# A fused attention and expert decoder on one core: in the first half of each slot, ScalarE takes the last half-slot's units out ahead of the exp instead of behind it

## The chip, the cores and the metric

The kernel runs on one core of one Trainium2 chip. The metric is the device time of one execution in microseconds (us). Three executions of the kernel before were timed; a fourth was profiled.

## The reference

The input is a batch of 8 sequences of 512 rows and 256 features, `x`, and a context of the same shape. Three layers follow each other, each with `x = layernorm(x + layer(x))`:

- a linear attention with a decaying state (decay 0.99, rate 0.01) of 128 features, which the kernel computes as a masked product of queries and keys;
- a cross attention on the context, with 16 heads of 16 features, softmax over 512 keys;
- a sum of a self attention of the same shape and a mixture of 8 experts (256 by 256 each), of which the two with the largest gate count.

All of it is float32.

## The kernel before, in words

Each sequence needs two softmax attentions of 16 heads: a cross attention (phase "C") and a self attention (phase "S"). `PHASES` puts the 16 phases in one row, and everything else is woven between them: the projections, layer norms, linear attention and experts of one sequence run while the softmax of another does. A phase is cut into 16 slots (4 groups of 4 heads, by 4 blocks of 128 keys), so there are 256 slots, and a slot has two halves, `h = 0` and `h = 1`, of two heads each. Time is counted in half-slots `t = 2 * s + h`; it starts at negative values, for the work that precedes the first softmax. "First half" below is `h = 0`, "second half" is `h = 1`.

Every engine runs its own loop over the same `t`, and issues its work in program order:

- TensorE (line 643 on): in each half the scores of two heads (`scores`: two matmuls side by side into the one buffer `sc`, which first wait for the exp of the half before, since `sc` is not doubled), then two matmuls for the row maxima of a slot six ahead (`max_tiles`, into `mx`, three banks in turn). In the first half follow the products of the last slot's probabilities with the values (`values`, eight matmuls into `op`). In the second half follow the **units**: all matmuls of everything that isn't softmax, each filling one of the two banks of `ms`.
- ScalarE (line 767 on): in each half the exp of the scores (`exps`, 128x1024, out of `sc` into `probs`, line 721), then the taking out of the units that carry the number of the half before (`UNITS.get(t - 1)`), then other tasks (`OTHERS["act"]`: the copy of `op` into `oT`, the last step of layer norms `apply01` and `apply23`, the gate's exp).
- VectorE: the maxima of `mx` (line 884), its own share of the units, layer norm statistics, the choice of experts. It takes the low part of the projections that are split into two (`low`, line 794), after ScalarE has made the high part (`high`, line 660).
- GpSimd adds the experts' outputs up (line 1051); SyncE issues the DMAs.

The order of units is written out by hand in the tables `LIN...`, `MID...` and `MOE...`: each name has a slot and a half. At most two units stand in one half. TensorE computes the units of both halves of a slot at one place, at the end of the slot's second half: first those with half 0, then those with half 1. ScalarE takes the units with half 0 out in the same slot's second half, behind that half's exp. It takes those with half 1 out in the first half of the next slot. The units with half 1 that ScalarE takes out are what the change moves. By the tables they stand in 148 of the 256 slots:

- one of the 16 expert units of a sequence (`moe`: 6 matmuls; taken out by two activations of 128x256 with a scale per row, line 714, into `moe`): 67 slots with that unit alone; in 14 more a `heads` unit (four transposes, VectorE takes them out) follows it on TensorE, in 6 `hT1` and in 6 `combT` (four transposes each, which ScalarE takes out with one copy, line 659);
- a projection of 128x512 that is taken out with a bias (`q1`, `k1`, `qc0`, `qc1`, `kc0`, `kc1`, `q3c0`, `q3c1`, `k3c1`, line 660): 42 slots with that unit alone (26 with four float32 matmuls, 16 with six float32r ones), 4 more with `heads` behind it;
- a copy of 128x512 alone (`o1`, `hT1`, `x2T1`, line 659): 9 slots.

A unit may only overwrite its bank of `ms` when the unit two before it has been taken out (`wait_unit_out` at the head of `unit`). An expert unit's taking out also waits until GpSimd has added the entry two before it (`acc`).

Of the kernel before, what the change touches and what calls it, by code (L numbers as in the profile page):

```python
# [37 lines left out]
PHASES = [("C", 0)] + [ph for n in range(B - 1) for ph in (("C", n + 1), ("S", n))] + [("S", B - 1)]  # L38
PHASE = {ph: p for p, ph in enumerate(PHASES)}
SLOTS = G * TB  # L40
# [59 lines left out]
def lin_at(task, n):  # L100

    slot, half = lin_table(n)[task]
    return 2 * (slot + (start_of("C", n) if n >= 2 else 0)) + half
# [111 lines left out]
def decoder(nc, x, xT, ctxT, w, out):  # L215
    with ExitStack() as ctx:
# [92 lines left out]
        def unit_bank(unit):  # L309
            return ms[:, PLACE[unit] % 2, :]  # L310

        def wait_unit(eng, *unit):

            eng.wait_ge(ms_t[PLACE[unit] % 2], PLACE[unit] // 2 + 1)
# [341 lines left out]
        def _(act):  # L656
            def copy(dst, src, bias=None):
                if bias is None:
                    return nc.scalar.activation(dst, src, ACT.Copy)  # L659
                return nc.scalar.activation(dst, src, ACT.Identity, bias=bias, scale=1.0)  # L660

            def high(task, n):

                name, c = task[0], int(task[-1])
                e = half_stack(task, n)
                bias = {"kc": W["bk2"], "qc": bq2, "k3": W["bk3"], "q3": bq3}[task[0:2]]
                if e >= 1:
                    act.wait_ge(stack_in[name], 16 * TERMS * SIDES * e)
                wait_unit(act, task, n)
                copy(part[name][:, 0, :].bitcast(F32R), unit_bank((task, n)), bias[:, c:c + 1]).then_inc(part_high[name], 1)  # L670

            def take_out(task, n):

                bank = unit_bank((task, n))
                done = ms_out[PLACE[task, n] % 2]
                if task in ("q1", "k1"):
                    if n >= 1:
                        wait_unit(act, "qc1", n - 1)
                    wait_unit(act, task, n)
                    copy(q1T if task == "q1" else k1T, bank, W["b" + task][:, 0:1]).then_inc(done, 1)  # L680
                elif task == "o1":
                    wait_unit(act, task, n)
                    copy(o1T[:], bank).then_inc(done, 1)
                elif task in ("x0", "x1"):
                    wait_unit(act, task, n)
                    copy(x1T[:, int(task[1]), :], bank).then_inc(done, 1)
                elif task in ("hT0", "hT1"):
                    wait_unit(act, task, n)
                    copy(headsT[:, int(task[2]), :], bank).then_inc(done, 1)
                elif task in ("x2T0", "x2T1"):  # L690
                    wait_unit(act, task, n)
                    copy(x2T_part[0][:, int(task[3]), :].bitcast(F32R), bank).then_inc(x2_high, 1)
                elif task == "gate":
                    wait_unit(act, task, n)
                    copy(gateT, bank[:, 0:P]).then_inc(done, 1)
                elif task == "combT":
                    wait_unit(act, task, n)
                    copy(combT, bank[0:E, :]).then_inc(done, 1)
                elif task in ("be0", "be1"):
                    k = ENTRY[task, n]  # L700
                    wait_unit(act, task, n)
                    if k >= 2:
                        act.wait_ge(acc, 2 * (k - 1))
                    copy(moe[:, k % 2, :], bank).then_inc(moe_out, 2)
                elif task.startswith("moe"):
                    k = ENTRY[task, n]
                    t, pair = int(task[3:]) // (E // 2), int(task[3:]) % (E // 2)
                    wait_unit(act, task, n)
                    act.wait_ge(g_step, G_STEPS * (n + 1))
                    if k >= 2:  # L710
                        act.wait_ge(acc, 2 * (k - 1))
                    for j in range(2):
                        e = 2 * pair + j
                        nc.scalar.activation(moe[:, k % 2, j * D:j * D + D], bank[:, j * D:j * D + D], ACT.Copy,  # L714
                                             scale=comb[:, t, e:e + 1]).then_inc(moe_out, 1)

            def exps(s, h):
                act.wait_ge(score, 2 * s + h + 1)
                if s - 1 + h >= 1:
                    act.wait_ge(pv, s - 1 + h)  # L720
                nc.scalar.activation(probs[:, (2 * s + h) % 3, :, :], sc[:], ACT.Exp).then_inc(exp_out, 1)  # L721

            def other(task, k, n):
                if task == "oT":
                    act.wait_ge(pv, TB * (k + 1))
                    if k >= 1:
                        wait_unit(act, "heads", k - 1)
                    copy(oT[:], op[:]).then_inc(oT_out, 1)
                elif task in ("apply01", "apply23"):
                    src, dst = ((x_s, x1), (x1b, x2[:, n % 2]))[k]  # L730
                    if k == 0 and n >= 1:
                        act.wait_ge(x1b_out, n)
                    if k == 1 and n == 0:
                        act.wait_ge(we_cut, 2 * DC)
                    if k == 1 and n >= 2:
                        act.wait_ge(y_out, 16 * (n - 1))
                    act.wait_ge(ln_step[k], LN_STEPS[k] * (n + 1))
                    for t in (0, 1) if task == "apply01" else (2, 3):
                        nc.scalar.activation(dst[:, t, :], src[:, t, :], ACT.Identity, bias=drop[:, k, t:t + 1],
                                             scale=rstd[:, k, t:t + 1]).then_inc(ln_out[k], 1)  # L740
                else:
                    act.wait_ge(g_step, G_STEPS * n + 3)
                    nc.scalar.activation(g_e[:], g_l[:], ACT.Exp).then_inc(g_exp, 1)
# [7 lines left out]
            for t in range(FIRST_HALF, LAST_HALF + 1):  # L751
                s, h = t // 2, t % 2
                if t == lin_at("y01", 0):
                    act.wait_ge(w_late, 16 * len(LATE))
                    nc.scalar.mul(bq2[:], W["bq2"][:], HD ** -0.5).then_inc(scaled, 1)
                    nc.scalar.mul(bq3[:], W["bq3"][:], HD ** -0.5).then_inc(scaled, 1)
                    nc.scalar.mul(W["wq2"][:], W["wq2"][:], HD ** -0.5).then_inc(scaled, 1)
                    act.wait_ge(w3_in, 16 * 2)
                    nc.scalar.mul(w3_stage[0][:, :, 0:D], w3_stage[0][:, :, 0:D], HD ** -0.5).then_inc(scaled, 1)
                    act.wait_ge(scaled, 4)  # L760
                if t == 2 * -12:
                    act.wait_ge(we_in, 16 * DC)
                    for c in range(DC):
                        copy(we_part[0][:, c, :].bitcast(F32R), we_stage[c]).then_inc(we_cut, 1)
                    for k in range(2):
                        copy(w3_part[0][:, :, W3_COLS[k]].bitcast(F32R), w3_stage[k]).then_inc(w3_cut, 1)
                if t == 0:
                    act.wait_ge(we_cut, 2 * DC)
                    act.wait_ge(w3_cut, 4)
                if 0 <= s < SLOTS * len(PHASES):  # L770
                    exps(s, h)
                for task, n in UNITS.get(t - 1, []):
                    if task in SPLITS:
                        high(task, n)
                    else:
                        take_out(task, n)
                for task, k, n in OTHERS["act"][t]:
                    other(task, k, n)
                if t == lin_at("qc0", 0) + 1:
                    act.wait_ge(fills, 5)  # L780
                    act.wait_ge(part_low["q"], 1)
                    for i in range(TERMS):
                        act.dma_start(qs[64 + HD * i:64 + HD * i + HD, 0, :, :],
                                      part["q"][64:128, Q_PART[i], :]).then_inc(stack_in["q"], 16)
# [346 lines left out]
```

## Time and profile before

| | |
|---|---|
| Three timed executions | 1293.77, 1296.06 and 1296.37 us, median 1296.06 us |
| Profiled execution | 1295.17 us, of which the span from the first to the last instruction is 1293.4 us |
| Granted TensorE clock, mean | 0.981 of full speed |
| TensorE matmul busy | 1224.4 us, 95% of the span |
| VectorE, ScalarE, GpSimd busy | 911.8, 776.9 and 348.4 us (70%, 60%, 27%) |
| Instructions | 19863 |

A busy time is a sum over the instructions of one engine, with overlaps counted once. Matmul ends are modelled. A row of the timeline gives the start in us from the span's start, the duration in us, the engine (PE is TensorE's matmuls, PEld its weight loads, ACT is ScalarE, DVE VectorE, POOL GpSimd), the line, the operation, the tiles as out<-in, their shapes and how many instructions are merged, and in brackets the idle time of the engine ahead of it and what ended that.

### The profile page before, as it was taken

Reading aid. Unit: us, or ns where it says so; the run is one execution under the profiler, and the core shown is the slowest. Engines: PE = TensorE matmul, PEld = TensorE weight load, DVE = VectorE, ACT = ScalarE, POOL = GpSimd, SP = SyncE. Lnnn points to the kernel's source line nnn. Section 1 sums busy time; section 2 is a strip of 40 time slices with the busy share of each in tenths; the row PEclk is TensorE's granted clock in tenths of the full one; section 3 lists DMA queues with packets and bytes.
Section 4 is the critical chain, followed back from the end, with each engine's and each line's share of the span. In section 5 each row is a group of like instructions: output and inputs, shape, how many; then the busy total and the mean of one; then the engine's idle time right before and its main releaser. Section 6 shows DMA issues by size and latency. Waiting matters only on the chain.

```text
span 1293.4 us, 19863 instructions
## 1 busy us (share of the span) xinstructions
PE 1224.4 (95%) x6912; PEld 603.1 (47%) x6912; DVE 911.8 (70%) x1825; ACT 776.9 (60%) x1081; POOL 348.4 (27%) x421
## 2 busy tenths in 40 slices
PE   7789989999999999999999999999999999997995
PEld 4333344454554445554554545544454444453542
DVE  5467777557776787767877687767777677767762
ACT  2235555656567665757657666676657576665664
POOL 2410012230622206211333206121152114420262
PEclk9879998999999999999999999999999999998998
DMA  6913324223334133333422243341323333303300
GB/s 234 146 28 63 60 33 59 49 27 73 61 67 67 23 72 57 67 51 50 83 43 58 35 83 51 66 67 26 60 49 51 51 51 51 67 2 51 50 19 17
DMA packets 50243, 74.92 MB, mean 58 GB/s; under 512 B 8536, under 2 KB 20320, under 8 KB 49888
## 3 DMA queue, kind: packets, MB, share of 16 engines
q1 hardware_dynamic: 48896, 72.72, 32.2%
q10 hardware_dynamic: 1248, 0.92, 0.4%
q8 instruction: 57, 0.93, 0.4%
q14 instruction: 42, 0.34, 0.1%
HBM read 18.04 MB, written 4.19 MB: 17 GB/s over the span
## 4 chain that ended last, share of the span: by engine, by line
PE 78%; DVE 9%; ACT 5%; issue 4%; DMA 2%; SPq 1%; POOL 0%; ACTq 0%; DVEq 0%
PE ms L422 36%; PE op L422 15%; PE sc L422 15%; PE mx L422 8%; DVE maxes L884 4%; ACT probs L721 2%; PE ms L527 2%; DMA qs<-q_parts 2%; PE ms L472 1%; ACT moe L714 1%; DVE ks L974 1%; SPq L370 1%; PE ms L522 1%; DVE x1b L835 1%; DMA qs<-shift_r 1%
## 5 line engine op out<-in xcount | busy, mean ns | idle before, releaser
L884 DVE TENSOR_REDUCE maxes<-mx 128x1 f32<-128x512 f32 x1024 | 657.7, 684 | 274.1 <-PE mx L422 272.1
L721 ACT ACTIVATE probs<-sc 128x1024 f32<-128x1024 f32 x512 | 524.9, 1025 | 390.7 <-PE sc L422 384.3
L1051 POOL TENSOR_TENSOR x<-x,moe 128x256 f32<-128x256 f32 x256 | 187.2, 731 | 688.4 <-ACT moe L714 668.5
L422 PE MATMUL op<-probs,v 128*32 128x512 f32 x2048 | 276.2, 612 | 1.7 <-ACT probs L721 1.1
L422 PE MATMUL sc<-qs,ks 50*128 50x512 f32 x1024 | 258.6, 502 | 15.8 <-ACT probs L721 10.2
L422 PEld LDWEIGHTS sc<-qs,ks 50*128 50x128 f32 x1024 | 96.2, 184 | 316.8 <-ACT probs L721 235.0
L422 PE MATMUL mx<-ks,qs 48*128 48x512 f32 x1024 | 208.8, 403 | 11.3 <-DVE maxes L884 6.7
L714 ACT ACTIVATE moe<-ms,comb 128x256 f32<-128x256 f32 x256 | 107.1, 473 | 27.3 <-PE ms L422 27.3
L422 PEld LDWEIGHTS mx<-ks,qs 48*128 48x128 f32 x1024 | 98.7, 189 | 17.8 <-DVE maxes L884 11.2
L422 PE MATMUL ms<-we_hi,x2T_hi 128*128 128x512 f32 x256 | 94.5, 450 | 3.0 <-DVE x1b L835 1.9
L422 PEld LDWEIGHTS op<-probs,v 128*32 128x32 f32 x2048 | 40.5, 108 | 95.7 <-issue 94.3
L422 PE MATMUL ms<-we_lo,x2T_hi 128*128 128x512 f32 x256 | 80.9, 397 | 0.0
L422 PE MATMUL ms<-we_hi,x2T_lo 128*128 128x512 f32 x256 | 80.9, 397 | 0.0
L422 PEld LDWEIGHTS ms<-we_hi,x2T_hi 128*128 128x128 f32 x256 | 39.5, 191 | 36.9 <-issue 17.4
L422 PEld LDWEIGHTS ms<-we_lo,x2T_hi 128*128 128x128 f32 x256 | 48.7, 190 | 11.5
L422 PEld LDWEIGHTS ms<-we_hi,x2T_lo 128*128 128x128 f32 x256 | 48.4, 189 | 11.7
L794 DVE SCALAR_TENSOR_TENSOR k_parts<-ms,w_bk,k_parts 128x512 fp32r<-128x512 f32 x32 | 24.0, 751 | 39.2 <-ACT k_parts L660 38.7
L1011 POOL TENSOR_SCALAR var<-mv 128x4 f32<-128x4 f32 x24 | 5.6, 234 | 146.8 <-DVE mv L915 146.1
L527 PE MATMUL ms<-w_ident,oT 128*128 128x128 f32 x256 | 39.7, 278 | 1.3 <-ACT oT L659 0.8
L660 ACT ACTIVATE k_parts<-ms,w_bk 128x512 fp32r<-128x512 f32 x32 | 22.0, 687 | 28.8 <-PE ms L422 28.8
L527 PEld LDWEIGHTS ms<-w_ident,oT 128*128 128x128 f32 x256 | 29.9, 141 | 19.9 <-DVE shift_r L848 12.5
L659 ACT ACTIVATE oT<-op 128x512 f32<-128x512 f32 x64 | 38.1, 596 | 1.2 <-PE op L422 1.2
(123 smaller groups left out, 1241.9 us busy)
## 6 DMA issues: line engine op xcount, KB each, us to landing
ks<-k_parts SPq DMA_DIRECT2D x192, 128.0 KB, 4.4
qs<-q_parts SPq DMA_DIRECT2D x189, 128.0 KB, 4.6
xT_s<-in_xT SPq DMA_DIRECT2D x8, 512.0 KB, 3.8
x_s<-in_x SPq DMA_DIRECT2D x8, 512.0 KB, 4.1
ctxT_s<-in_ctxT SPq DMA_DIRECT2D x8, 512.0 KB, 3.8
out<-x SPq DMA_DIRECT2D x7, 512.0 KB, 2.9
qs<-shift_r SPq DMA_DIRECT2D x128, 8.0 KB
probs<-in_we SPq DMA_DIRECT2D x1, 1024.0 KB, 7.2
```

Of the source, the lines that this page charges most:

```text
L370: sp.dma_start(dst[at:at + HD, e % RING, :, :], part[name][64 * side:64 * side + 64, which[r], :]).then_inc(stack_in[name], 16)
L422: return nc.tensor.matmul(dst, lhsT, rhs, start=first, stop=last, skip_group_check=True)
L472: last = nc.tensor.transpose(bank[:, t * P:(t + 1) * P], src[:, t, c * P:(c + 1) * P], ident[:])
L522: last = nc.tensor.transpose(bank[0:SHIFT * HG * TB, 0:P], shift_n[:, n % 2].rearrange("p s a m -> p (s a m)"), ident[:])
L527: last = nc.tensor.transpose(bank[:, t * P:t * P + P], oT[:, t * P:t * P + P], ident[:])
L659: return nc.scalar.activation(dst, src, ACT.Copy)
L660: return nc.scalar.activation(dst, src, ACT.Identity, bias=bias, scale=1.0)
L714: nc.scalar.activation(moe[:, k % 2, j * D:j * D + D], bank[:, j * D:j * D + D], ACT.Copy, scale=comb[:, t, e:e + 1]).then_inc(moe_out, 1)
L721: nc.scalar.activation(probs[:, (2 * s + h) % 3, :, :], sc[:], ACT.Exp).then_inc(exp_out, 1)
L794: nc.vector.scalar_tensor_tensor(out=part[name][:, 1, :].bitcast(F32R), in0=unit_bank((task, n)), scalar=bias[:, c:c + 1], in1=part[name][ ...
L884: nc.vector.tensor_reduce(maxes[:, g % 2, at:at + 1], mx[:, i % 3, :], AX_X, ALU.max).then_inc(max_out, 1)
L1051: nc.gpsimd.tensor_tensor(x2[:, n % 2, t, :], x2[:, n % 2, t, :], moe[:, k % 2, j * D:j * D + D], ALU.add).then_inc(acc, 1)
```

## The change

In the first half of each slot the loop of ScalarE takes the units of the last half-slot out first and issues the exp behind them. In the second half the order stays: exp, then units. The other tasks stay behind both. No other engine's program changes.

```diff
@@ -767,13 +767,15 @@
                 if t == 0:
                     act.wait_ge(we_cut, 2 * DC)
                     act.wait_ge(w3_cut, 4)
-                if 0 <= s < SLOTS * len(PHASES):
+                if h == 1 and 0 <= s < SLOTS * len(PHASES):
                     exps(s, h)
                 for task, n in UNITS.get(t - 1, []):
                     if task in SPLITS:
                         high(task, n)
                     else:
                         take_out(task, n)
+                if h == 0 and 0 <= s < SLOTS * len(PHASES):
+                    exps(s, h)
                 for task, k, n in OTHERS["act"][t]:
                     other(task, k, n)
                 if t == lin_at("qc0", 0) + 1:
```

## Rows read from the trace of the kernel before

**Rows 1.** The chain that ended last, shares of the span by engine.

```profile
PE 78%; DVE 9%; ACT 5%; issue 4%; DMA 2%; SPq 1%; POOL 0%; ACTq 0%; DVEq 0%
```

**Rows 2.** Waits, whole span: total us, times, longest.

```profile
POOL x L1051 <- ACT moe L714: 668.5, 100, 33.4
...
PEld sc L422 <- ACT probs L721: 235.0, 286, 1.5
...
PEld ms L422 <- DVE q_parts L794: 10.2, 16, 3.4
```

**Rows 3.** Timeline, slot 57: its first half, an expert unit ahead of it.

```profile
359.98 0.63 PE L422 MATMUL ms<-we_lo,x2T_hi 128*128 128x512 f32 x2
...
360.54 0.50 PE L422 MATMUL sc<-qs,ks 50*128 50x512 f32 x2
...
361.09 1.02 ACT L721 ACTIVATE probs<-sc 128x1024 f32<-128x1024 f32 x1 [1.40 <-PE sc L422]
...
361.21 1.07 PE L422 MATMUL op<-probs,v 128*32 128x512 f32 x8
...
362.01 0.84 ACT L714 ACTIVATE moe<-ms,comb 128x256 f32<-128x256 f32 x2
...
362.21 0.50 PE L422 MATMUL sc<-qs,ks 50*128 50x512 f32 x2
```

**Rows 4.** Timeline, slot 254, near the end: a first half without max matmuls.

```profile
1275.36 1.06 PE L422 MATMUL op<-probs,v 128*32 128x512 f32 x8
1275.47 1.02 ACT L721 ACTIVATE probs<-sc 128x1024 f32<-128x1024 f32 x1 [0.60 <-PE sc L422]
...
1276.55 0.50 PE L422 MATMUL sc<-qs,ks 50*128 50x512 f32 x2
```

**Rows 5.** Timeline, slot 51: ScalarE waits for an expert unit of half 0.

```profile
334.03 0.62 PE L422 MATMUL ms<-we_lo,x2T_hi 128*128 128x512 f32 x2
...
334.69 0.84 ACT L714 ACTIVATE moe<-ms,comb 128x256 f32<-128x256 f32 x2 [0.81 <-PE ms L422]
```

**Rows 6.** Timeline, slot 34: ScalarE waits for a projection of half 0.

```profile
249.37 1.45 PE L422 MATMUL ms<-ctxT_s,w_wk 128*128 128x512 f32 x3
...
250.92 0.69 ACT L660 ACTIVATE k_parts<-ms,w_bk 128x512 fp32r<-128x512 f32 x1 [1.21 <-PE ms L422]
```

**Rows 7.** Timeline, slot 48: a projection of half 1, taken out behind the exp.

```profile
314.79 1.98 PE L422 MATMUL ms<-xT_s,w_wk 128*128 128x512 f32 x4
...
318.17 0.68 ACT L660 ACTIVATE x1T<-ms,w_bk 128x512 f32<-128x512 f32 x1
...
318.74 0.23 ACT L743 ACTIVATE g_e<-g_l 128x32 f32<-128x32 f32 x1
```

**Rows 8.** Timeline, slot 69: an expert unit and hT1, both of half 1.

```profile
413.73 0.63 PE L422 MATMUL ms<-we_lo,x2T_hi 128*128 128x512 f32 x2
...
414.20 0.60 PE L472 MATMUL ms<-w_ident,heads 128*128 128x128 f32 x4
...
416.19 0.83 ACT L714 ACTIVATE moe<-ms,comb 128x256 f32<-128x256 f32 x2
...
416.90 0.61 ACT L659 ACTIVATE lin<-ms 128x512 f32<-128x512 f32 x1
...
417.38 1.05 ACT L721 ACTIVATE probs<-sc 128x1024 f32<-128x1024 f32 x1
```

**Rows 9.** Timeline, slot 63: the late exp of the second half, and the scores behind it.

```profile
391.01 1.03 ACT L721 ACTIVATE probs<-sc 128x1024 f32<-128x1024 f32 x1
...
391.24 0.63 PE L422 MATMUL ms<-we_lo,x2T_hi 128*128 128x512 f32 x2
392.09 0.49 PE L422 MATMUL sc<-qs,ks 50*128 50x512 f32 x2 [0.22 <-ACT probs L721]
```

**Rows 10.** Timeline, slot 229: layer norm steps behind the taking out of an expert unit.

```profile
1164.49 2.07 ACT L739 ACTIVATE x<-x1b,drop,rstd 128x256 f32<-128x256 f32 x4
...
1166.70 1.06 PE L472 MATMUL ms<-w_ident,x 128*128 128x128 f32 x8 [1.99 <-ACT x L739]
```

## The prediction

> **What bounds the kernel now.** I read the chain that ended last first: 78% of it is TensorE, 5% ScalarE [rows 1]. The waits come next: TensorE's weight loads for scores waited 286 times for an exp, 235.0 us in total, and that is its largest wait [rows 2]. A weight load can wait while the matmuls ahead of it still stream, so only a timeline tells whether this is lost time.
>
> The timeline of a first half [rows 3] has the whole cycle. Write S for the start of its scores, 360.54. The exp starts at S+0.55 and ends at S+1.57, and the scores of the second half start at S+1.67. The value matmuls between them are modelled to end at 362.28. The same rows show where scores start when TensorE alone decides: 0.07 before the modelled end of the matmuls ahead (expert unit: end 360.61, scores 360.54). By this TensorE is free at 362.21, which is when the second scores start. Near the end of the kernel the row maxima are finished, and the value matmuls end earlier (at 1276.42, so TensorE is free at 1276.35); there the scores start at 1276.55, 0.06 after the exp's end of 1276.49 [rows 4]. From the exp's start to the scores this takes 1.08, in slot 57 1.12. So in the first half **two limits lie 0.04 to 0.05 apart**: TensorE's own work at S+1.67, and behind it the exp's round trip at S+1.62. An exp later than today by d moves the next scores by d less 0.045. TensorE's program is a fixed row behind these scores, so the slot ends later by the same.
>
> In the second half TensorE has units to compute, usually 1 to 3 us of them, so that exp has room.
>
> **The change, part by part.** *Nothing is added or removed*: the same activations run, and no DMA or semaphore changes its place against another engine's program. Moved are the units of half 1 that ScalarE takes out, in 148 slots; in the other 108 the order stays. They now stand ahead of the exp of the first half, on which the weight loads of the next scores wait; they no longer stand between the first exp and the second.
>
> *When can taking out begin?* An expert unit's activation starts 0.04 after the modelled end of its last matmul (334.65 to 334.69) [rows 5]. One with a bias as a column starts 0.10 after it (250.82 to 250.92) [rows 6]. The unit ends 0.07 past S, since scores start that much ahead of the modelled end. So an expert unit is ready at S+0.11, a projection at about S+0.165, a copy at S+0.11, all before the scores themselves are ready for exp at S+0.545.
>
> *How long does it hold ScalarE?* Two expert activations: 416.19 to 416.90, a step of 0.71. A copy: 416.90 to 417.38, 0.48 up to an exp's start [rows 8]. A projection with bias: 318.17 to 318.74, 0.57 [rows 7].
>
> The Trainium skill ("ScalarE: Activation LUTs", What ACT_TABLE_LOAD costs) gives an activation 186 ns and 0.833 ns per element, 93 ns more for a column operand, and an overlap of 93 ns between neighbours. By it the step of one 256-wide expert activation is an estimated 0.40, so 0.80 for two, where the row has 0.71; the sum below would be about 7 us higher. The measured step is used.
>
> The sum, by kinds of slot (counts from the tables):
> - 67 with an expert unit alone: 0.11 + 0.71 = S+0.82 in place of 0.545, 0.275 later, less 0.045: 0.23 each, 15.4 us.
> - 12 with an expert unit and then hT1 or combT: the expert unit ends at 414.36 and its taking out 0.75 later, at 415.11; the copy takes it to 415.59. S is 414.80 less 0.07, 414.73, so the exp is due at 415.27 and comes 0.32 late [rows 8]. combT is a narrower copy, 0.04 less. About 0.25 each after the cover, 3.0 us.
> - 42 projections alone: 0.165 + 0.57 = S+0.735, 0.19 late, 0.145 after the cover; 41 of them count (one, q1 of the third sequence, ended early because TensorE waited for a DMA), 5.9 us. The unit of rows 7 shows the same: end 316.77, ready 316.87, done 317.44, where the exp was due at 317.25.
> - 9 copies alone: 0.11 + 0.48 = 0.59, 0.045 late, all of it covered: 0.
> - 18 with `heads` behind: the unit ends with 0.44 less, ready at S-0.33, done by S+0.38, before the scores: 0.
>
> That is 24.3 us, and 0.1 more for three slots at the end that have no cover [rows 4].
>
> *What comes back.* The second exp no longer stands behind these units. Where layer norm steps also stood ahead of it, it was late, but it was TensorE's limit in only five slots like slot 63: the exp of 391.01 to 392.04 set the scores at 392.09, while the matmuls ahead end at 391.87, so TensorE would be free at 391.80 [rows 9]. That is 0.29 each, 1.5 us. In slot 229 the four layer norm steps start at 1164.49, and TensorE waits 1.99 for them [rows 10]. Today exp and two expert activations stand ahead of them; then it is the same three, but begun at S+0.11 by the expert pair in place of S+0.545 by the exp. So the steps start 0.435 earlier, and the slot gains this in place of losing 0.23, 0.7 us. High parts done earlier let VectorE's low parts start about 0.1 earlier where TensorE waits for them behind a `heads` unit, four slots, 0.4 us; all such waits of weight loads are 10.2 us, the upper bound [rows 2]. In all 2.6 us.
>
> *Costed at nothing.* VectorE: after its two maxima of a first half it waits for no one but the high part, which comes earlier; the maxima of the second half shift with TensorE. GpSimd: it waits 668.5 us for expert results, so they come earlier into an idle engine [rows 2]; the taking out of a unit waits for the entry two before it, and no row shows ScalarE waiting for that. If that cover were gone, the exp would wait as well: one addition's length each time. SyncE: some stacks of keys and queries can be issued earlier, by at most what VectorE's queue lets through, 0.1. ScalarE's waits now stand ahead of exp: a projection also waits for the DMAs of its predecessor, several slots old.
>
> Sum: 24.4 - 2.6 = **21.8 us more**. The profiled execution took 1295.17, 0.9 under the median of 1296.06. From it follows 1317.0, from the median 1317.9. I forecast 1318.
>
> **The bounds.** If the cover of 0.045 is not there (the row's 362.21 could be the exp's round trip after all, with 0.05 more for a queue), 120 slots cost 0.045 more and the nine copies appear: 1324. If it is twice that, 1312. If taking out can start at the modelled end itself, minus 0.04 to 0.10 a slot, 1311; both together, 1306. If no overlap between activations remained (0.84 + 0.11 for the pair [rows 3], 0.68 for a projection), 0.13 and 0.11 more, 1333.
>
> **The rivals.**
> 1. *Hidden.* The taking out fits between the unit's end and the scores' end, so the exp is not late. For it: ScalarE is idle 1.40 ahead of this exp in slot 57 [rows 3], and busy only 60% of the span. Against it: the idle time lies before S+0.11, when no unit is ready, and only 0.43 remain for a step of 0.71. It would hold if units were ready 0.23 earlier. Then only the gains stand: 1296.06 - 2.6 = 1293.5, within 0.2%. The Trainium skill ("Perfetto Trace Analysis", Identifying the Most-Contended Engine) has the engine with the highest occupancy decide; by that, an order on an engine busy 60% changes nothing. Rows 3 speak against that rule here, since the path passes from scores through exp to scores within a half.
> 2. *Faster.* The late second exps are the price paid today: 12 slots like slot 69 (0.45 late), 12 like slot 63 (0.95), and slot 229 (1.9) are 18.7 us. If TensorE waited in all of them and rival 1's condition holds too, 1277. It decides from the point where a second half's units are shorter than the exp's lateness. Against it: the brackets that name ScalarE stand only in slots like those of rows 9 and 10; in the other 19 of these 25 TensorE still computes units when the late exp ends.
> 3. *Heavier.* The exp behind a taking out does not overlap it and pays a semaphore's delay too: 0.24 more in 79 slots, 0.11 more in 41, 0.12 in the rest, 25 us more, 1343. Rows 8 speak against it: an exp follows a copy with a step of 0.48, where the copy takes 0.61.
>
> **How the numbers follow.** About 0.2% (2.6 us) is what a measurement of this kernel can tell from no change. Forecast 0.80 (1306 to 1328), heavier 0.11, hidden 0.06, faster 0.03. So slower 0.91, same 0.06, faster 0.03. The range is 1308 to 1328: it leaves out the faster and hidden cases, most of the heavier one, and the thin ends of my own.
>
> **What would show it.** In slots with an expert unit alone, the exp of the first half starts 0.82 after the scores, directly behind two activations of line 714, and the next scores at S+1.90 in place of 1.67; with a projection S+1.81; without a unit, or with `heads` behind, S+1.67 as before. The exp of the second half starts 0.55 after its scores in nearly all slots. TensorE's matmul busy time stays near 1224 and its waits for exp grow by some 22 us. Rival 1 would show the exp at S+0.55, rival 3 at S+0.95 or later, and either makes the forecast wrong. So would a row in which ScalarE, ahead of the exp, waits for GpSimd or a DMA.

## The result and the profile after

| | before | after |
|---|---|---|
| Four executions, median | 1296.12 us (1293.77 to 1296.37) | 1313.85 us (1311.09 to 1318.42) |
| Profiled execution / its span | 1295.17 / 1293.4 us | 1311.09 / 1309.2 us |
| ScalarE busy | 776.9 us | 784.7 us |

The ratio is 1.0144, with a 95% interval of 1.0113 to 1.0176. The change makes the kernel 17.7 us slower. Executions at a lower granted clock, one of the kernel before (1363.27 us) and one of the last version below (1871.21 us), are left out of all medians and ratios.

The beginning and the end of an execution differ from run to run: the first scores come between 72.8 and 79.3 us after the start in the ten traces, whatever the order. So I also compare a stretch in which this hardly occurs, called the stretch below: from the first scores of slot 27 to the first scores of slot 229. The windows view gives its bounds and length, and then busy time of TensorE's matmuls, its weight loads, VectorE, ScalarE and GpSimd (instructions in brackets), the granted clock as a share of full speed, and the DMA share and rate. First the kernel before, then the changed one:

```profile
207.18:1162.32 955.14, 942.19 (x5453) 471.04 (x5452) 700.84 (x1421) 611.71 (x861) 276.76 (x343) 1.00 0.32 54
```

```profile
203.36:1175.91 972.55, 946.21 (x5451) 469.49 (x5451) 701.24 (x1421) 616.89 (x861) 276.51 (x343) 1.00 0.32 53
```

The same work at the same full clock takes 17.4 us more, and TensorE is busy in only 4.0 of these.

The chain that ended last, by engine, and four lines of the waits of the changed kernel (total us, times, longest):

```profile
PE 65%; ACT 15%; DVE 11%; issue 7%; DMA 1%; SPq 0%; POOL 0%; ACTq 0%; DVEq 0%
```

```profile
ACT probs L721 <- PE sc L422: 266.0, 336, 6.5
...
PEld sc L422 <- ACT probs L721: 258.7, 282, 1.6
...
ACT moe L714 <- PE ms L422: 86.6, 109, 1.8
...
PE sc L422 <- ACT probs L721: 25.1, 91, 1.1
```

ScalarE's share of the chain went from 5% [rows 1] to 15%, TensorE's from 78% to 65%. The weight loads of scores wait 23.7 us more for an exp than in [rows 2], and the score matmuls themselves 25.1 where it was 10.2 us. The two lines overlap in time and are not to be added. ScalarE waits less for scores than before (it was 384.3 us) and more for expert units (it was 27.3): it now meets a unit first.

The timeline of slot 57, to be laid beside [rows 3]:

```profile
358.83 0.63 PE L422 MATMUL ms<-we_lo,x2T_hi 128*128 128x512 f32 x2
...
359.39 0.50 PE L422 MATMUL sc<-qs,ks 50*128 50x512 f32 x2
...
359.50 0.84 ACT L714 ACTIVATE moe<-ms,comb 128x256 f32<-128x256 f32 x2 [0.97 <-PE ms L422]
...
360.06 1.06 PE L422 MATMUL op<-probs,v 128*32 128x512 f32 x8
360.23 1.02 ACT L721 ACTIVATE probs<-sc 128x1024 f32<-128x1024 f32 x1
...
361.30 0.49 PE L422 MATMUL sc<-qs,ks 50*128 50x512 f32 x2 [0.18 <-ACT probs L721]
```

With S = 359.39, the expert pair starts at S+0.11, the exp at S+0.84 instead of S+0.55, and the next scores at S+1.91 instead of S+1.67. The value matmuls now end at 361.12, 0.18 before these scores. TensorE waits for the exp.

The first half with a projection ahead (slot 48, S = 314.68), where the exp comes at S+0.75 and the next scores at S+1.82:

```profile
314.68 0.50 PE L422 MATMUL sc<-qs,ks 50*128 50x512 f32 x2
...
314.85 0.69 ACT L660 ACTIVATE x1T<-ms,w_bk 128x512 f32<-128x512 f32 x1 [1.59 <-PE ms L422]
...
315.43 1.02 ACT L721 ACTIVATE probs<-sc 128x1024 f32<-128x1024 f32 x1
...
316.50 0.50 PE L422 MATMUL sc<-qs,ks 50*128 50x512 f32 x2
```

And slot 69, with an expert unit and hT1 ahead, beside [rows 8]. Its S is 414.77, so the exp comes at S+0.88 and the next scores at S+1.96:

```profile
414.24 0.60 PE L472 MATMUL ms<-w_ident,heads 128*128 128x128 f32 x4
...
414.44 0.84 ACT L714 ACTIVATE moe<-ms,comb 128x256 f32<-128x256 f32 x2 [0.21 <-PE ms L422]
...
415.17 0.60 ACT L659 ACTIVATE lin<-ms 128x512 f32<-128x512 f32 x1
...
415.65 1.03 ACT L721 ACTIVATE probs<-sc 128x1024 f32<-128x1024 f32 x1
...
416.73 0.50 PE L422 MATMUL sc<-qs,ks 50*128 50x512 f32 x2 [0.23 <-ACT probs L721]
```

**Where the time went, over all slots.** I compared each half of each slot, from scores to scores, between the two traces. In slots with a moved unit the first halves are 25.9 us longer in all and the second halves 7.0 us shorter. The rest (slots without a moved unit, the start, and the second halves of slots 12 and 22, whose waits differ from run to run) is 3.1 us shorter. The sum is 15.8, which is the difference of the two spans.

What the second halves give back has two main sources. The first is the late exp, as in slot 63. Here it starts at 390.05 and no longer sets the scores, which follow the expert unit's modelled end of 391.61 by -0.07 as TensorE does when it decides alone (in [rows 9] they were held until 0.05 after the exp):

```profile
390.05 1.01 ACT L721 ACTIVATE probs<-sc 128x1024 f32<-128x1024 f32 x1
...
390.98 0.63 PE L422 MATMUL ms<-we_lo,x2T_hi 128*128 128x512 f32 x2
...
391.54 0.50 PE L422 MATMUL sc<-qs,ks 50*128 50x512 f32 x2
```

The second I had mostly missed, and slot 68 shows it. Its second half begins at 411.37 before and at 411.69 after. Before:

```profile
411.89 0.75 DVE L794 SCALAR_TENSOR_TENSOR q_parts<-ms,bq2s,q_parts 128x512 fp32r<-128x512 f32 x1
...
412.03 0.66 PE L472 MATMUL ms<-w_ident,heads 128*128 128x128 f32 x4
...
412.69 0.30 PEld L422 LDWEIGHTS ms<-we_hi,x2T_hi 128*128 128x128 f32 x2 [0.24 <-DVE q_parts L794]
412.69 0.72 PE L422 MATMUL ms<-we_hi,x2T_hi 128*128 128x512 f32 x2
```

After:

```profile
411.85 0.74 DVE L796 SCALAR_TENSOR_TENSOR q_parts<-ms,bq2s,q_parts 128x512 fp32r<-128x512 f32 x1
...
412.36 0.65 PE L472 MATMUL ms<-w_ident,heads 128*128 128x128 f32 x4
...
412.77 0.72 PE L422 MATMUL ms<-we_hi,x2T_hi 128*128 128x512 f32 x2
```

The transposes start 0.67 after the second scores in both. The expert unit follows them by 0.66 before and by 0.41 after. It needs the bank that the projection filled, and before the change VectorE's low part still read that bank until 412.64. The low part waits for ScalarE's high part, so when the high part comes earlier the bank does too. Eleven slots gain 0.26 to 0.37 by this, 3.1 us. Slots 250 and 251 gain 0.27 and 0.30 by a bank too: in slot 251 before, the expert unit starts 0.73 after the second scores and its bracket names the taking out of the expert unit ahead (line 714, 0.23 us); after, it starts 0.43 behind them.

**Six pairs that start late.** A unit that is ready at S+0.11 isn't taken out before ScalarE is free. In six of the 67 slots with an expert unit alone, layer norm steps of the half before still hold it. In slot 42 (S = 288.20) the pair starts at S+0.41, the exp at S+1.13, and the half costs 0.55:

```profile
287.63 1.08 ACT L739 ACTIVATE x<-x1b,drop,rstd 128x256 f32<-128x256 f32 x2
...
288.61 0.83 ACT L714 ACTIVATE moe<-ms,comb 128x256 f32<-128x256 f32 x2
...
289.33 1.03 ACT L721 ACTIVATE probs<-sc 128x1024 f32<-128x1024 f32 x1
```

In slot 74 and four like it the pair starts at S+0.18 and the exp at S+0.89, and each costs 0.30.

### The profile page after: what moved, and what is told of

It is laid out like the page before. It is cut to its first block, busy times and chain, and to the rows that moved or that the text cites. A ratio compares the mean times of both kernels' runs of the same rounds, so it can differ in the third digit from the quotient of the medians.

```text
span 1309.2 us, 19863 instructions
## 1 busy us (share of the span) xinstructions
PE 1225.3 (94%) x6912; PEld 598.4 (46%) x6912; DVE 912.0 (70%) x1825; ACT 784.7 (60%) x1081; POOL 348.2 (27%) x421
## 4 chain that ended last, share of the span: by engine, by line
PE 65%; ACT 15%; DVE 11%; issue 7%; DMA 1%; SPq 0%; POOL 0%; ACTq 0%; DVEq 0%
PE ms L422 36%; PE sc L422 12%; ACT probs L721 10%; PE op L422 7%; PE mx L422 6%; DVE maxes L886 5%; ACT moe L714 3%; PE ms L527 2%; PE ms L472 1%; DVE ks L976 1%; PE ms L522 1%; ACT x L739 1%; DMA qs<-q_parts 1%; DMA qs<-shift_r 1%; DVE x1b L837 1%
## 5 line engine op out<-in xcount | busy, mean ns | idle before, releaser
L422 PE MATMUL sc<-qs,ks 50*128 50x512 f32 x1024 | 258.0, 500 | 32.5 <-ACT probs L721 25.1
L422 PEld LDWEIGHTS ms<-we_hi,x2T_lo 128*128 128x128 f32 x256 | 48.2, 188 | 11.5
```

Of the source, the lines that this page charges most:

```text
L422: return nc.tensor.matmul(dst, lhsT, rhs, start=first, stop=last, skip_group_check=True)
```

## The experiments

The reason to be tested: a first half has two limits, 0.04 apart (the cover), and a taking out ahead costs as much as it makes the exp later, less the 0.04. The rivals are that something else in the moved order costs (banks, queues, the second halves), or that these extra microseconds come from other engines.

**Only the expert units ahead.** The other units stay behind the exp. The edit is against the kernel before; `...` marks lines left out of a diff.

```diff
+                units = UNITS.get(t - 1, [])
+                ahead = [u for u in units if h == 0 and u[0].startswith('moe')]
+                for task, n in ahead:
...
                 if 0 <= s < SLOTS * len(PHASES):
                     exps(s, h)
-                for task, n in UNITS.get(t - 1, []):
+                for task, n in units:
+                    if (task, n) in ahead:
+                        continue
```

> Only the expert units go ahead of the exp; the other units of half 1 stay behind it. Theory (round trip): the exp starts when the taking out ends, and only what exceeds a cover of about 0.05 us reaches the next scores. 67 slots with an expert unit alone: exp at S+0.83, next scores at S+1.91, 0.25 us each, 16.6 us; the 26 slots with another unit behind it: 0. Back come 1.5 us in the five slots like 63 and 0.7 of slot 229 (0.25 of it counted above). Span 14 to 15 us over the kernel before. Rival (cost spread over all moved units alike, by disturbance of TensorE or by waits ahead of the exp): 93 of 160 moved units, so about 9 us, and some of it in slots with heads behind the unit.

One execution took 1309.80 us, one of the kernel before 1292.86. The span is 14.6 us over that of the trace before, as the theory had it, and the stretch takes 966.64 us, 11.5 more. The 67 first halves with an expert unit alone have a median of 1.912 with the exp at S+0.835, as with the whole change, and cost 17.25 us together. Those with a projection are back at 1.663 to 1.667. Where hT1 follows the expert unit, the half costs nothing either: the expert pair is out before the scores are, and only the copy behind it, which here stands behind the exp, had delayed the exp.

**All but the expert units ahead.** Against the last one:

```diff
-                ahead = [u for u in units if h == 0 and u[0].startswith('moe')]
+                ahead = [u for u in units if h == 0 and not u[0].startswith('moe')]
```

> All units but the expert units go ahead; these stay behind the exp. Theory (round trip): 41 projections alone cost 0.155 us each, 6.4 us; copies alone, and hT1 or combT behind an expert unit, reach S+0.60 for the exp and cost 0.01. Back come 0.27 in each of the 12 slots after qc0 or qc1 (the next unit's bank is free earlier) and about 0.2 in the four with heads behind the projection, 4 us. Together 2 to 3 us over the kernel before. Rival (cost spread alike over all moved units): 67 of 160, 6 to 7 us.

One execution took 1299.52, the kernel before 1292.86, which is 6.7 less. By itself that would suit the rival. The stretch takes 956.81, only 1.7 more. The span is 4.4 us over the trace before (the traced execution before was itself 2.3 us slower than the 1292.86 here), and 2.4 of these lie in slot 230, where the granted clock was 0.50 from 1168.4 to 1171.5 us in this run and 1.00 in the trace before; there the exp stands at S+0.83 and S+0.84 in the two halves. The projections cost 0.155 to 0.16 each, with the exp at S+0.753 and the half 1.822 long. A copy puts the exp at S+0.60 and costs 0.01. The bank wait of slot 68 is gone here too (-0.27 in ten slots, -0.37 in the one after kc1), and so it belongs to the projections. Together the two runs give 13.2 us in the stretch, the whole change 17.4. What is missing is above all in the slots with two moved units: neither part of the change alone costs anything where hT1 follows an expert unit, but the two together cost 1.8 us there; and of the six slots in which combT follows one, the first part gains 0.28 in four and the second in all six, the whole in one.

**Half an expert unit ahead.** Only the first of its two activations stands ahead of the exp; the second and all other units stay behind.

```diff
+                units = UNITS.get(t - 1, [])
+                split = h == 0 and 0 <= s < SLOTS * len(PHASES) and len(units) > 0 and units[0][0].startswith("moe")
+                if split:
+                    take_out(*units[0], parts=(0,))
                 if 0 <= s < SLOTS * len(PHASES):
                     exps(s, h)
-                for task, n in UNITS.get(t - 1, []):
...
+                for task, n in units:
+                    if split and (task, n) == units[0]:
+                        take_out(task, n, parts=(1,))
```

> Only the first of the two activations of each expert unit goes ahead of the exp; everything else stays as before. Theory (round trip): it ends at S+0.11+0.36 = S+0.47, before the scores are ready for the exp at S+0.545, so the exp and the next scores stay at S+0.545 and S+1.66 in all 67 slots; five slots like 63 gain up to 0.3 and slot 229 gains 0.36: 1 to 2 us under the kernel before. Rival (what is taken out ahead costs in proportion): half of 17 us, 8 us more.

One execution took 1290.60, the kernel before 1292.86; the stretch takes 951.65, 3.5 less than before. Slot 57, S = 359.64:

```profile
359.64 0.50 PE L422 MATMUL sc<-qs,ks 50*128 50x512 f32 x2
...
359.74 0.48 ACT L715 ACTIVATE moe<-ms,comb 128x256 f32<-128x256 f32 x1 [0.97 <-PE ms L422]
...
360.18 1.03 ACT L722 ACTIVATE probs<-sc 128x1024 f32<-128x1024 f32 x1
...
361.10 0.47 ACT L715 ACTIVATE moe<-ms,comb 128x256 f32<-128x256 f32 x1
361.30 0.50 PE L422 MATMUL sc<-qs,ks 50*128 50x512 f32 x2
```

One activation fits between the unit's end and the scores' end: the exp starts at S+0.54 and the next scores at S+1.66. Taking units out ahead costs nothing as long as it ends before the scores do. Slot 42 is the one of the 67 where it doesn't: behind the layer norm steps the single activation puts the exp at S+0.78, and the half costs 0.19. The gains remain: 0.31 in the five slots like 63, 0.36 in slot 229, 0.28 in six combT slots; the last had not been foreseen. This separates the lateness of the exp from everything else that the order changes.

**More of the same cost.** The changed kernel, with one spare copy of 128x96 between the expert pair and the exp in the 67 slots.

```diff
+                    mine = [task for task, _ in UNITS.get(t - 1, [])]
+                    if len(mine) == 1 and mine[0].startswith("moe"):
+                        nc.scalar.activation(spare[:], ident[:, 0:96], ACT.Copy)
                     exps(s, h)
```

> The change, with one more activation (a copy of 128x96 into a spare tile, which nothing reads) between the taking out and the exp in the 67 slots with an expert unit alone. Theory (round trip): past the cover each ns of lateness is one of the slot. The copy takes a step of about 0.17 us, so exp at S+1.0, next scores at S+2.08, 67 times 0.17 = 11 us over the changed kernel, all of it in these first halves. Rival (TensorE has work to fill, the first halves stretch less than the exp is late): under 6 us.

One execution took 1329.37, the kernel before 1292.86. The 67 first halves have a median of 2.084, 0.172 more than with the change alone, 11.5 us in all, which is what the theory asked for. The stretch, in which 56 of them lie, takes 981.04, 8.5 more than with the change alone (9.6 in these halves, less 1.1 that combT slots gain). The whole execution is longer by more because its first scores came 6.4 us later, ahead of everything that the edit touches. Slot 57, S = 368.03:

```profile
368.03 0.50 PE L423 MATMUL sc<-qs,ks 50*128 50x512 f32 x2
...
368.86 0.28 ACT L781 ACTIVATE spare<-w_ident 128x96 f32<-128x96 f32 x1
369.04 1.02 ACT L722 ACTIVATE probs<-sc 128x1024 f32<-128x1024 f32 x1
...
370.11 0.50 PE L423 MATMUL sc<-qs,ks 50*128 50x512 f32 x2 [0.35 <-ACT probs L722]
```

The exp is 0.174 later than with the change alone, and the next scores 0.172: past the cover, lateness passes on in full. The points of exp and next scores lie on one line: S+0.753 and 1.821, 0.835 and 1.912, 0.875 and 1.96, 1.009 and 2.084, always 1.07 to 1.085 apart. A copy, with 0.600 and 1.671, stands at the foot of this line (1.071 apart), and 0.541 with 1.663 (1.122 apart) is on the flat part ahead of it. With 1.077 from exp to scores, the cover is 1.663 - 1.077 - 0.543 = 0.043; the spread of the line leaves 0.035 to 0.05.

**Only what is free or pays.** Of each expert unit the first activation stands ahead, the whole unit where `heads` follows or where layer norm steps wait (slot 229 and its like); other units stand ahead only where `heads` follows and for `qc0` and `qc1`, which end the bank wait at a cost of 0.16.

```diff
+                        full = units[-1][0] == "heads" or (task, n) == ("moe15", B - 2)
+                        take_out(task, n, (0, 1) if full else (0,))
...
+                    elif (units[-1][0] == "heads" or task in ("qc0", "qc1")) and not behind:
```

> Only what costs nothing goes ahead of the exp: the first activation of each expert unit, the whole expert unit or projection where heads stands behind it and in slot 229, and qc0 and qc1. Theory (round trip): first halves stay at 1.66 us except the 12 with qc0 or qc1, 0.155 longer; back come 1.5 us (slots like 63), 0.43 (slot 229), 0.27 in each of 12 slots after qc0 or qc1, 0.6 behind heads, and 0.28 in six slots with combT, as in the run with the first activation alone. Together 5 to 6 us under the kernel before, ratio 0.995 to 0.997. Rival (these single gains are lost again at the next wait): within 1 us of the kernel before.

The median of twelve executions is 1288.94 us, that of 26 of the kernel before 1295.55, ratio 0.9958 with an interval of 0.9940 to 0.9975; the stretch takes 950.87, 4.3 less than before. The gains hold, and the rival's 1 us lies outside the interval.

**More cover for the exp.** TensorE issues both pairs of row maxima of a slot (VectorE reads them; their scores are six slots ahead) in the first half instead of one in each, in the slots that have a unit for ScalarE and units of their own (136 of them still have maxima to compute; the expectation says 137). This makes the first half longer by TensorE's own work and the second shorter. It was run on the order of before and on the changed order.

```diff
-                if 0 <= s + MAX_LEAD < SLOTS * len(PHASES):
+                if 0 <= s + MAX_LEAD < SLOTS * len(PHASES) and not (h == 1 and both):
...
+                if h == 0 and both and 0 <= s + MAX_LEAD < SLOTS * len(PHASES):
+                    max_tiles(4 * (s + MAX_LEAD) + 2)
```

On the order of before:

> The kernel before, with the row maxima of the second half computed by TensorE already behind the values of the first half, in 137 slots that have a moved unit and enough units in the second half. Theory (two limits in a first half): TensorE's own work there becomes 0.34 longer, 2.0 us, and the second half 0.34 shorter, so the time stays within 2 us of the kernel before. Rival (VectorE can't free the third bank in time, and TensorE waits for it): 0.1 or more in each of the 137, over 10 us more.

The median of ten executions is 1293.87 us, ratio to before 0.9979 (0.9961 to 0.9996), so within the 2 us; the stretch takes 952.25, 2.9 less than before. 2.7 us of this come from 18 slots (54, 58, 62 and their like, 0.13 to 0.16 each); their cause was not looked into. On the changed order:

> The change with the same move of the row maxima. Theory (the cost of the change is the exp's round trip exceeding TensorE's work in the first half): the trip ends at S+1.91 with an expert unit and S+1.83 with a projection, TensorE's work at S+2.0, so the cost of 0.25 and 0.155 is gone in these slots and only the gains stay: 3 to 6 us under the run with the row maxima moved alone, where the change was 16 to 18 us over the kernel before. Rival (taking out ahead costs something of its own on TensorE or VectorE): still 10 us or more over that run.

The median of ten executions is 1288.91 us, ratio 0.9953 (0.9934 to 0.9973); the stretch takes 948.45. Slot 57 of it, S = 358.42:

```profile
358.42 0.50 PE L427 MATMUL sc<-qs,ks 50*128 50x512 f32 x2
...
359.26 1.02 ACT L730 ACTIVATE probs<-sc 128x1024 f32<-128x1024 f32 x1
...
360.09 0.50 PE L427 MATMUL mx<-ks,qs 48*128 48x512 f32 x2
...
360.43 0.40 PE L427 MATMUL sc<-qs,ks 50*128 50x512 f32 x2
```

The exp is as late as in the changed kernel, S+0.84, and the scores don't wait for it: they come at S+2.01 in both of these kernels, set by the maxima matmuls ahead of them. The weight loads of scores wait for an exp about half as long as in the changed kernel, and as long as with the row maxima moved alone (122.4 us), so the late exp adds nothing to them:

```profile
PEld sc L427 <- ACT probs L730: 123.2, 152, 1.7
```

So the same edit on ScalarE that costs 17.7 us on the kernel before gains 5.0 us (1293.87 to 1288.91, stretch 3.8; the intervals of the two ratios just overlap) once TensorE has other work in that place. Of the 3.8, 2.4 come in the six combT slots, where GpSimd never holds VectorE up in this run (see the last section). This is the clearest sign that the exp's lateness past TensorE's own work is the cost. In slot 42, where the exp is at S+1.13, its round trip still ends behind that work, and the half is 0.21 longer than with the row maxima moved alone.

**Both.** The paired maxima with half an expert unit ahead, and the other units ahead in paired slots. Against the picked version, without the row maxima's edit:

```diff
-                    elif (units[-1][0] == "heads" or task in ("qc0", "qc1")) and not behind:
+                    elif (units[-1][0] == "heads" or paired(s)) and not behind:
```

> The row maxima moved as in the last two, all projections and copies of these slots ahead of the exp, of the expert units the first activation (the whole where heads is behind). Theory: no first half is longer than TensorE's 2.0 us, all gains come: about 0.27 each after qc0 and qc1 without their cost of 0.155, so 2 us under the version that picks without moving the maxima, 7 to 8 us under the kernel before. Rival (the moved maxima make VectorE late): over the picked version.

The median of five executions is 1284.79 us, ratio 0.9921 (0.9895 to 0.9946); the stretch takes 945.95, 9.2 less than before. It beats the kernel before by 0.8%, and the changed one, timed apart from it, by 2.2%. It is 4.2 us under the picked version, where 2 were expected: the 2.9 that moving the maxima gains by itself had been left out. It is 4.1 us faster than the changed order with the same pairs, though the intervals of the two ratios overlap; the stretch has 2.5 of this.

## Why the prediction was right, and where a step was off

The forecast was 1318 with a range of 1308 to 1328; it is 1313.85. The mechanism held: exp and next scores stand where they were forecast, to 0.02, in nearly all slots. The losses were slightly too small and the gains much too small:

| step | predicted | measured |
|---|---|---|
| 67 expert units alone | 0.23 each, 15.4 | exp S+0.835, 0.25 each, but 0.30 in five and 0.55 in one, 17.2 |
| 6 with hT1 | 0.25 each | exp S+0.875, 0.30 each, 1.8 |
| 6 with combT | 0.25 each | 0.01 each |
| projections alone | 0.145 each, 5.9 | exp S+0.753, 0.155 to 0.16 each, 6.6 |
| copies alone | 0 | 0.01 each |
| 18 with `heads` behind | 0 | 0 |
| five second halves like slot 63 | -0.29 each | -0.31 each |
| slot 229, net | -0.435 | -0.43 |
| low parts, bank waits | -0.4 | -3.1 in 11 slots, -0.6 in 3 with `heads` |
| slots 250 and 251 | 0 | -0.6 together |
| cover | 0.045 | 0.043 |

- **The cost.** 24.4 against 25.9 us, and the closeness is in part luck. Two things made it too small. Every late exp costs 0.01 to 0.05 more than forecast, some 2.4 us in all: the expert pair, for one, starts at S+0.11 and steps 0.73 to the exp, where 0.71 had been taken from a row in which a copy follows. And the six pairs that start late add 0.6 us; the prediction let every pair start at S+0.11 and did not ask what ScalarE does then. One term was too large, combT's, by 1.5 us. The estimate of 0.80 for the pair's step, which the prediction works out from the Trainium skill ("ScalarE: Activation LUTs", What ACT_TABLE_LOAD costs), would have given an exp at S+0.91; the measured step was the better term.
- **combT was the largest wrong cost.** The prediction took combT like hT1. But combT transposes the expert weights that VectorE chooses, and ScalarE's pair needs the same weights. Both wait for VectorE long before these scores, as slot 50 (S = 323.95) shows, so there the pair is nearly out when the scores start:

```profile
323.36 0.84 ACT L714 ACTIVATE moe<-ms,comb 128x256 f32<-128x256 f32 x2 [0.98 <-DVE comb L971]
323.43 0.60 PE L564 MATMUL ms<-w_ident,comb 128*8 128x128 f32 x4 [0.28 <-DVE comb L971]
...
324.09 0.57 ACT L659 ACTIVATE o1T<-ms 8x512 f32<-8x512 f32 x1
...
324.57 1.00 ACT L721 ACTIVATE probs<-sc 128x1024 f32<-128x1024 f32 x1
```

- **What comes back: 2.6 predicted, 7.0 measured, the step that failed in size.** "High parts done earlier let VectorE's low parts start about 0.1 earlier where TensorE waits for them behind a `heads` unit, four slots, 0.4 us" had the mechanism and not its extent. Beside the three with `heads` the wait sits in 11 slots, which gain 0.26 to 0.37 each. The prediction gave its upper bound, 10.2 us, from the waits [rows 2], and then took a count from the tables instead of looking at some of those 16 waits in the timeline. Waits for a bank that ScalarE itself holds (slots 250 and 251, and the combT slots of the runs with a part of the change) were not in the sum at all.
- **Slot 229** went as worked out. The steps start 1.74 after S, and TensorE waits 1.31 for them instead of 1.99 [rows 10], which gives back 0.68 where the first half lost 0.25:

```profile
1177.65 2.07 ACT L739 ACTIVATE x<-x1b,drop,rstd 128x256 f32<-128x256 f32 x4
...
1179.87 0.85 PE L472 MATMUL ms<-w_ident,x 128*128 128x128 f32 x6 [1.31 <-ACT x L739]
```

- **The sum** of mechanisms is 25.9 - 7.0 = 18.9, where 21.8 was predicted; the medians differ by 17.7. The other 1.2 is within what executions differ by at their start and end.
- **The rivals.** *Hidden* needed an exp at S+0.55; in the 67 slots it starts at S+0.84. The half expert unit shows that this rival holds up to one activation. *Faster* needed TensorE waiting in all slots with a late second exp; of these it did in those like slot 63 and 229 alone. *Heavier* needed an exp at S+0.95 or later; only slot 42 has one, and there it is the late start of the pair and no longer step. The prediction also named a row in which ScalarE waits for GpSimd or a DMA ahead of the exp as a sign against it; none stands ahead of the exp of a first half; ScalarE's waits for DMAs lie ahead of the first scores, and the expert pairs that wait for VectorE (slot 50 and its like) do so well before. The rule that the prediction cites beside *hidden* from the Trainium skill ("Perfetto Trace Analysis", Identifying the Most-Contended Engine), that the engine with the highest occupancy decides, would as read there have kept the time; here an order on an engine busy 60% cost 1.4%.
- **TensorE's busy time** stayed, 1225.3 us against 1224.4.

## What to carry to other kernels

Before putting work ahead of a step, lay the two limits of the stage on one time axis (when the waiting engine is free by its own work, and when the step's round trip ends); their distance is what the order may cost for nothing, and past it every nanosecond is multiplied by the number of rounds. Reordering is not all or nothing: a unit that is taken out by two instructions can have one of them in each gap, and work of the waiting engine that isn't urgent can be moved to where it waits. Where a class of waits has a bound larger than the effect that is claimed for it, look at a few of its members in the timeline before taking a smaller number.

## What the runs showed of the hardware that was not expected

A GpSimd addition can hold VectorE up for its whole length, and in these traces a few nanoseconds decide whether it does. In slot 50 of the changed kernel the earlier expert pair moves GpSimd's second addition onto VectorE's last step for the row maxima:

```profile
324.79 0.73 POOL L1053 TENSOR_TENSOR x<-x,moe 128x256 f32<-128x256 f32 x1
...
324.79 0.76 DVE L896 SCALAR_TENSOR_TENSOR shift_n<-maxes,shift_n 128x16 fp32r<-128x16 f32 x1
...
326.64 0.28 PE L522 MATMUL ms<-w_ident,shift_n 128*32 128x128 f32 x1
```

VectorE's operation, 0.18 us in most slots, takes 0.76 and ends with the addition. TensorE's unit for it comes at S+2.69, where it was S+2.35 before, and this eats the 0.28 that these slots gain where VectorE isn't held: 1.4 us in five slots. In slot 82 of the kernel with only the expert units ahead the two meet as well, and VectorE is not held:

```profile
479.02 0.77 POOL L1060 TENSOR_TENSOR x<-x,moe 128x256 f32<-128x256 f32 x1
...
479.02 0.18 DVE L903 SCALAR_TENSOR_TENSOR shift_n<-maxes,shift_n 128x16 fp32r<-128x16 f32 x1
```

Four of the ten traces have such meetings within 13 ns, 21 in all, and they fall into two kinds. In nine, GpSimd's record starts 5 to 11 ns ahead of VectorE's: VectorE takes 0.76 us and GpSimd 0.73 to 0.74. In twelve, GpSimd's record starts at most 3 ns ahead, or up to 13 ns behind: VectorE takes 0.17 to 0.18 and GpSimd 0.76 to 0.78, some 0.04 more. All five meetings of the changed kernel with the row maxima moved are of the second kind.

The Trainium skill ("SBUF — State Buffer", Who interferes with whom) has VectorE and GpSimd share a pair of ports: a VectorE instruction with two inputs in SBUF contends there with a GpSimd instruction that reads SBUF, and the order of issue decides who blocks. The traces agree with both: VectorE stands still for GpSimd's length in one order, and GpSimd loses 0.04 in the other. In slot 82 the records have GpSimd ahead by 3 ns and VectorE isn't blocked; so if issue order decides, it can't be read from records that close. Between 3 and 5 ns no meeting was seen, and no run separates the two further.
